# Attention and a routed expert layer on one core: the expert slots written out in place of a loop, and the router's logits computed transposed in four column strips

## The reference

```python
# attention: 16 heads of 16 channels, causal, on layernorm(x) and ctx
qp, kp = elu(q) + 1, elu(k) + 1
out[t] = qp[t] @ sum_{s <= t} outer(kp[s], v[s])      # per head
x = x + (out / cumsum(qp)) @ Wo + bo
# router and experts on layernorm(x), called hidden
h      = relu(hidden @ W1 + b1)          # 256 -> 128
logits = h @ W2 + b2                     # 128 -> 8
sel    = argmax(softmax(logits))         # one expert per token
x      = x + hidden @ expert_W[sel] + expert_b[sel]
```

## Time and profile before

| | before |
|---|---|
| median of 3 runs | 1158.4 us |
| the profiled execution: span | 1158.5 us |
| first part, to the last `place` | 0 to 943 us |
| tables for the slots | 943 to 960 us |
| slots | 960 to 1158.5 us |
| busy over the span | PE 90%, DVE 73%, POOL 51%, ACT 49% |

### The profile page before, as it was taken

How to read it: one execution, slowest core, us unless ns; L and a number is a source line. 1 busy time by engine, 2 the same in 40 slices (tenths; PEclk the granted TensorE clock), 3 DMA queues, 4 the chain that set the end, 5 groups by cost and what they waited for, 6 DMA issues and landing times.

```text
span 1158.5 us, 39374 instructions
## 1 busy us (share of the span) xinstructions
PE 1044.3 (90%) x15828; PEld 727.5 (63%) x15829; DVE 843.8 (73%) x1739; ACT 562.7 (49%) x945; POOL 587.0 (51%) x682
## 2 busy tenths in 40 slices
PE   2989999999999999999999999999999626999996
PEld 1666666666666666666667666666667414666664
DVE  2688887887888887878878788888877643555554
ACT  2544544454555544554455545445444114666664
POOL 4144444544444455554555444544444444777766
PEclk9989999999999999999999999999999857999999
DMA  3823333333333333333334333333322014666664
GB/s 104 241 75 93 94 93 94 93 93 93 94 93 95 97 97 97 101 101 100 107 104 120 97 93 93 93 93 93 93 76 76 30 51 138 193 190 184 195 185 135
DMA packets 88601, 127.11 MB, mean 110 GB/s; under 512 B 13693, under 2 KB 67584, under 8 KB 88320
## 3 DMA queue, kind: packets, MB, share of 16 engines
q1 hardware_dynamic: 75392, 89.98, 30.1%
q0 software_dynamic: 13056, 34.90, 7.9%
HBM read 73.03 MB, written 36.06 MB: 94 GB/s over the span
## 4 chain that ended last, share of the span: by engine, by line
PE 23%; issue 23%; POOL 18%; DMA 13%; SPq 7%; ACT 5%; DVE 4%; DVEq 0%; POOLq 0%; ACTq 0%
DMA x_res<-in_x 8%; PE b_a L808 8%; POOL buckets L409 7%; PE b_b L1014 6%; SPq L338 5%; POOL x_res L433 3%; DMA stage<-buckets 2%; DMA out<-stage 2%; PE b_b L855 2%; PE b_a L1005 2%; ACT x2n L494 2%; POOL row L419 2%; PE b_a L803 2%; PE b_b L813 2%; ACT x2T L506 1%
## 5 line engine op out<-in xcount | busy, mean ns | idle before, releaser
L581 DVE TENSOR_TENSOR stage<-b_s,causal 128x1024 f32<-128x1024 f32 x192 | 226.1, 1219 | 47.6 <-PE b_s L835 37.1
L461 POOL DMA_INDIRECT out<-stage x136 | 136.6, 1005 | 59.2 <-issue 30.2
L409 POOL DMA_INDIRECT buckets<-row,place x128 | 140.8, 1100 | 34.6 <-issue 34.6
L1014 PE MATMUL b_b<-we_sb,x3T 128*128 x544 | 150.5, 400 | 0.0
L808 PE MATMUL b_a<-xnT,wq_sb 128*128 128x512 f32 x256 | 128.0, 624 | 7.4 <-ACT x2T L506 5.1
L539 ACT ACTIVATE x3n<-stage 128x256 f32<-128x256 f32 x136 | 81.5, 599 | 88.4 <-DMA stage<-buckets 83.8
L813 PE MATMUL b_b<-wo_sb,attT 128*128 128x256 f32 x512 | 121.4, 391 | 2.4 <-DVE attT L681 2.4
L494 ACT ACTIVATE x2n<-row 128x256 f32<-128x256 f32 x128 | 66.5, 590 | 115.5 <-POOL row L425 115.5
L407 POOL TENSOR_TENSOR onehots<-onehots,onehot 128x32 bf16<-128x32 bf16 x32 | 7.8, 244 | 223.6 <-DVE place L614 223.6
L808 PE MATMUL b_a<-ctxT,wk_sb 128*128 128x512 f32 x256 | 118.4, 605 | 1.8 <-ACT pos L480 1.8
L813 PE MATMUL b_b<-wv_sb,ctxT 128*128 128x256 f32 x512 | 119.0, 385 | 0.0
(11 more groups left out here) (119 smaller groups left out, 1954.4 us busy)
## 6 DMA issues: line engine op xcount, KB each, us to landing
stage<-buckets SPq DMA_DIRECT2D x136, 130.0 KB, 2.2
x_in<-in_x SPq DMA_DIRECT2D x32, 512.0 KB, 5.1
ctxT<-in_ctx SPq DMA_DIRECT2D x32, 512.0 KB, 6.3
qsel<-qp SPq DMA_DIRECT2D x256, 64.0 KB
x_res<-in_x SPq DMA_DIRECT2D x32, 512.0 KB, 7.3
out<-stage POOLq DMA_INDIRECT x136
we_sb<-in_L_ffn_expert_W SPq DMA_DIRECT2D x8, 256.0 KB, 6.0
buckets<-row,place POOLq DMA_INDIRECT x128
```

Source lines behind the costliest of these rows:

```text
L409: pool.indirect_dma_start(buckets, bass.IndirectOffsetOnAxis(place[:, slot(route), t:t + 1], 0), row[:, slot(route), t, :], None).then_inc ...
L461: pool.indirect_dma_start(out.rearrange("t p n -> (t p) n"), bass.IndirectOffsetOnAxis(rows2[:, r, TOKEN:TOKEN + 1].bitcast(U32), 0), sums ...
L581: dve.tensor_tensor(dst.rearrange("p g h s q -> p g (h s) q"), b_s[:, :, 256 * t:256 * t + 256].rearrange("p g (a q) -> p g a q", q=C), ca ...
L1014: last = pe.matmul(b_b[:, h, 0:D], x3T[:, h, P * k:P * k + P], we_sb[:, k, bass.ds(e, 1), :], start=(k == 0), stop=(k == KC - 1))
```

## The change

1. The loop over slots becomes a straight program: the same `step` calls, with plain numbers where the loop variable was. Registers with the slots' rows and experts are still read eight at a time.
2. The router's second product is turned round. `w2_wide` (8 columns of W2 and 24 columns of zeros) is the stationary operand, `hT` of a tile the moving one, and the four tiles go to the four strips of 32 PSUM partitions. ACT adds the bias on the way to `logitsT`, PE transposes that once (128x128) between the two halves of `wo`, and DVE takes maximum and marks straight from PSUM, without its bias add.
3. Around it: `b2` is loaded as four columns of 8 rows, behind the experts' weights; two memsets and one copy on DVE build `bias_2` and `w2_wide`.

```diff
         def slot_schedule(eng, step, begin=lambda first, how_many: None):
-            begin((0, -2), RING)
-            for j in range(RING):
-                step(*((0, j - k) if j - k >= 0 else None for k in range(3)))
-            with eng.Fori(1, SLOTS // RING, 1) as i:
-                begin((i, -2), RING)
-                for v in range(RING):
-                    step(*((i, v - k) for k in range(3)))
-            begin((SLOTS // RING, -2), 2)
-            for j in range(SLOTS, SLOTS + 2):
-                step(*((j // RING, j % RING - k) if j - k < SLOTS else None for k in range(3)))
+            for j in range(SLOTS + 2):
+                if j % RING == 0:
+                    begin((j // RING, -2), RING if j < SLOTS else 2)
+                step(*(((j - k) // RING, (j - k) % RING) if 0 <= j - k < SLOTS else None for k in range(3)))
...
+                sp.wait_ge(s_cst, MADE)
+                for t in range(GT):
+                    sp.dma_start(bias_2[R * t:R * t + E, :], b2.rearrange("(n o) -> n o", o=1)).then_inc(s_eld, 16)
...
+                if merge:
+                    act.wait_ge(s_lg, n(merge, k=1))
+                    if group_no(merge) == 0:
+                        act.wait_ge(s_eld, EXPERTS)
+                    else:
+                        act.wait_ge(s_lgTp, n(merge))
+                    act.activation(logitsT[:, :], b_s[:, 0, 0:P], ACT.Identity, bias=bias_2[:, :]).then_inc(s_lgT, 1)
...
+            dve.tensor_copy(w2_wide[:, 0:E], w2_sb[:, :]).then_inc(s_w2, 1)
...
-                        dve.wait_ge(s_pick, n(merge, 5))
-                    dve.wait_ge(s_lg, n(merge, k=1))
-                    dve.tensor_tensor(logits[:, :, :], b_s[:, 0, 0:GT * E].rearrange("p (t e) -> p t e", e=E),
-                                      per_expert(bias_2[:, :]), ALU.add).then_inc(s_pick, 1)
-                    dve.wait_ge(s_pick, n(merge, 5, 1))
-                    dve.tensor_reduce(top[:, :], logits[:, :, :], axis=AX.X, op=ALU.max).then_inc(s_pick, 1)
+                        dve.wait_ge(s_pick, n(merge, 4))
+                    dve.wait_ge(s_lgTp, n(merge, k=1))
+                    scored = b_s[:, 0, P:2 * P].rearrange("p (t e) -> p t e", e=R)[:, :, 0:E]
+                    dve.tensor_reduce(top[:, :], scored, axis=AX.X, op=ALU.max).then_inc(s_pick, 1)
...
             def logit_products():
                 for t in range(GT):
-                    last = pe.matmul(b_s[:, 0, E * t:E * t + E], hT[:, P * t:P * t + P], w2_sb[:, :],
+                    last = pe.matmul(b_s[strip(t), 0, 0:P], w2_wide[:, :], hT[:, P * t:P * t + P],
                                      start=True, stop=True)
                 return last
...
-                if attend:
-                    for b in range(2):
+                for b in range(2):
+                    if attend:
                         pe.wait_ge(s_att, n(attend, 2, 1 + b))
                         for t in range(b, GT, 2):
                             last = tokens_first(b_b[:, b, D * (t // 2):D * (t // 2) + D], attT, wo_sb, t)
                         last.then_inc(s_y, 1)
+                    if merge and b == 0:
+                        pe.wait_ge(s_lgT, n(merge, k=1))
+                        pe.transpose(b_s[:, 0, P:2 * P], logitsT[:, :], ident[:, :]).then_inc(s_lgTp, 1)
```

More of the change, by code:

```diff
@@ L37, in build @@
     RING = 8
-    WEIGHTS = 16 * 14
-    EXPERTS = 16 * (E + 1)
+    WEIGHTS = 16 * 13
+    EXPERTS = 16 * (E + 1 + GT)
     POOL_MADE = 22
-    MADE = 12
+    MADE = 14
     FILL_STEPS = E + 3 + 3 * (E - 1) + 4
@@ L79, in build @@
         bias_1 = sb("bias_1", [FF, 1])
-        bias_2 = sb("bias_2", [P, E])
+        bias_2 = sb("bias_2", [P, 1])
         bias_e = sb("bias_e", [P, E, D])
@@ L87, in build @@
         w2_sb = sb("w2_sb", [FF, E])
+        w2_wide = sb("w2_wide", [FF, R])
         we_sb = sb("we_sb", [P, KC, E, D])
@@ L117, in build @@
         hT = sb("hT", [FF, N])
+        logitsT = sb("logitsT", [P, P])
         logits = sb("logits", [P, GT, E])
@@ L203, in build @@
         s_hT = sem("s_hT")
+        s_w2 = sem("s_w2")
         s_lg = sem("s_lg")
+        s_lgT = sem("s_lgT")
+        s_lgTp = sem("s_lgTp")
         s_pick = sem("s_pick")
@@ L298, in load_weights @@
                                      b[P * k:P * k + P].rearrange("(p o) -> p o", o=1)).then_inc(s_wld, 16)
-                for dst, b, wide in ((bias_v, bv, D), (bias_o, bo, D), (bias_2, b2, E)):
+                for dst, b, wide in ((bias_v, bv, D), (bias_o, bo, D)):
                     sp.dma_start(dst[:, :],
@@ L567, in _ @@
             dve.memset(slot_e[:, :], 0.0).then_inc(s_cst, 1)
+            dve.memset(bias_2[:, :], 0.0).then_inc(s_cst, 1)
+            dve.memset(w2_wide[:, :], 0.0).then_inc(s_cst, 1)
             dve.wait_ge(s_cst, MADE)
             dve.wait_ge(s_wld, WEIGHTS)
+            dve.tensor_copy(w2_wide[:, 0:E], w2_sb[:, :]).then_inc(s_w2, 1)
             def of_mask(which):
@@ L686, in step @@
                     if group_no(merge) >= 1:
-                        dve.wait_ge(s_pick, n(merge, 5))
-                    dve.wait_ge(s_lg, n(merge, k=1))
-                    dve.tensor_tensor(logits[:, :, :], b_s[:, 0, 0:GT * E].rearrange("p (t e) -> p t e", e=E),
-                                      per_expert(bias_2[:, :]), ALU.add).then_inc(s_pick, 1)
-                    dve.wait_ge(s_pick, n(merge, 5, 1))
-                    dve.tensor_reduce(top[:, :], logits[:, :, :], axis=AX.X, op=ALU.max).then_inc(s_pick, 1)
-                    dve.wait_ge(s_pick, n(merge, 5, 2))
-                    dve.tensor_tensor(tied[:, :, :], logits[:, :, :], per_tile(top[:, :]), ALU.is_equal)\
-                        .then_inc(s_pick, 1)
-                    dve.wait_ge(s_pick, n(merge, 5, 3))
+                        dve.wait_ge(s_pick, n(merge, 4))
+                    dve.wait_ge(s_lgTp, n(merge, k=1))
+                    scored = b_s[:, 0, P:2 * P].rearrange("p (t e) -> p t e", e=R)[:, :, 0:E]
+                    dve.tensor_reduce(top[:, :], scored, axis=AX.X, op=ALU.max).then_inc(s_pick, 1)
+                    dve.wait_ge(s_pick, n(merge, 4, 1))
+                    dve.tensor_tensor(tied[:, :, :], scored, per_tile(top[:, :]), ALU.is_equal).then_inc(s_pick, 1)
+                    dve.wait_ge(s_pick, n(merge, 4, 2))
                     dve.tensor_tensor(logits[:, :, :], tied[:, :, :], per_expert(iota_m8[:, :]), ALU.mult)\
                         .then_inc(s_pick, 1)
-                    dve.wait_ge(s_pick, n(merge, 5, 4))
+                    dve.wait_ge(s_pick, n(merge, 4, 3))
                     dve.tensor_reduce(first[:, :], logits[:, :, :], axis=AX.X, op=ALU.min).then_inc(s_pick, 1)
-                    dve.wait_ge(s_pick, n(merge, 5, 5))
+                    dve.wait_ge(s_pick, n(merge, 4, 4))
                     if group_no(merge) >= 1:
@@ L795, in _ @@
             pe.wait_ge(s_wld, WEIGHTS)
+            pe.wait_ge(s_w2, 1)
             def strip(g):
```

## The result

| | time (us) | before on the same chip | ratio, 95% interval |
|---|---|---|---|
| changed kernel | 1171.5 | 1158.5 | 1.0107, 1.0087 to 1.0128 |

The changed kernel is slower by 13 us; its profiled execution took 1171.0 us, with a span of 1169.2. The forecast was 1162.5, 9 us too low, with the time inside the range of 1154 to 1174: + 4 was said and + 13 came.

What follows compares the result with a forecast made beforehand. The prediction took a closed chain through PE, DVE and POOL to bound each step. From 1158.5 us, + 0.5 (first merge) + 5.6 (28 steps) - 2 (slots) gave 1162.6, stated as 1162.5, range 1154 to 1174.

Steps and rivals of the forecast that it cites:

- rival B: Steps: no pull on POOL, L425 stays 8.29 us behind `place`, 0.51 us lost per step; 1171 us, chance 0.18.
- A's steps: Steps in the forecast's own case: masks and `kp` pull POOL forward, 0.20 us lost each; 1159 to 1166, chance 0.50.
- F: Slots: streamed instructions stall the engines beside full DMA queues, 1.4 us per 8 slots; 1185, or 1174 at half; chance 0.09.
- The closed chain: Steps: each waits in a ring from `attT` through `wo`, `row`, `place`, POOL, `x2n` and attention sums to `attT`; 27.8 us.
- The late `qp`: Steps: `qp` 1.4 us later also delays SP's DMAs and moves `x_res` for POOL's L433; costed at nothing.
- The saving on PE swallowed by `attT`: Logits on PE: PE free 0.6 us earlier, but `wo` then waits for `attT`; gain 0 to 0.1 us, taken as 0.
- The rule of the Trainium skill: Logits on PE: swap operands and tile by columns when the moving side has 32 columns or fewer; 18 us in all.
- `place` 0.51 us late: DVE in a step: transpose behind half of `wo` delays `top`, `qp` and both `row` adds; `place` at 433.44 instead of 432.93.
- `kp` pulls POOL forward: DVE and POOL: masks and `kp` start only 0.20 us later, so L425 and `x2n` come 0.20 us later, not 0.51.
- 28 x 0.20 = 5.6 us: First part: each of 28 steps gets 0.20 us longer, 5.6 us in all; bounds per step 0.11 and 0.51.
- The slots, - 2 us: Slots: dropping the loop's jumps saves 0.3 us at 15 borders, half reaching POOL; about 2 us, bounds 0 and 7.8.

Runs made afterwards that it cites:

- eight more operations: Kernel before plus eight small chained DVE operations, output unused, behind `onehot` and ahead of `qp` in each step: 1205.1 us against 1189.8.
- two turns: Kernel before with its slot loop over 16 slots instead of 8, leaving out every second jump back: 1158.7 us against 1159.6.
- the router's half: Changed kernel with the old loop over slots put back: 1198.6 us against 1189.8 before, and 1198.9 against 1189.4 on a second chip.
- the straight half: Kernel before with only its slots written out straight: 1182.8 us against 1189.8, 1183.3 against 1189.4, and 1163.8 against 1159.6 on three chips.
- the one with `kp` later: Kernel before with the first `kp` of a step moved behind the second masks on DVE: 1203.2 us against 1189.8.

## Why the prediction was right or wrong

- **The number.** + 13 came where + 4 was forecast. The first part lost 7.9 us for a forecast of 5.6, and the slots lost 4.7 where they were to win 2. The 1171.5 measured is what rival B gives (1171), but that is luck: B says that the scale stays 8.29 us behind `place`, and it came to 7.82. What happened is A's steps and, for the slots, something of F.
- **The closed chain** of `attT`, `wo`, `row`, `place`, POOL, `x2n` was right: a usual step is longer by what its parts changed, + 0.62 and - 0.47, and the remaining 14.13 us did not move. The late `qp` cost nothing, as taken, though it did move POOL's L435 by 1.9 us (446.23): there it runs beside the whole of `u`, which takes 3.13 us instead of 1.73, and DVE still has 1.60 us to wait for PE ahead of `attT`.
- **The saving on PE swallowed by `attT`** was right: 0.62 us less for the logits, and PE's idle time before `wo` 15.1 us over 32 steps, where before had 2.4. The rule of the Trainium skill (TensorEngine Tiling (Array Packing), "Performance Considerations") was worth 18 us in the prediction, 0.6 us a step; PE's own time for the logits did fall, from 1.05 to 0.43 us, but PE wasn't what the step waited for.
- **`place` 0.51 us late**: 0.62, all of the difference ahead of `top`. It started 2.96 us behind `attT`, where I had 2.84: `wo` 0.75 behind `attT` (0.80), the transpose 1.83 behind that (1.71), `top` 0.38 behind its start (0.33).
- **`kp` pulls POOL forward**: right, and stronger, 0.47 instead of 0.31. The run with eight more operations shows the same 1.07 us DMA with the old router, so this is shown and not only argued. POOL's DMA ended 1.49 us behind the start of `kp`, as the prediction had read from two steps.
- **28 x 0.20 = 5.6 us**: 7.9, and 9.3 to 10.8 on the other kind of chip. The usual step lost 0.15 or 0.16 (there 0.19), less than taken, so 4.4 us; what I left out is that a step which falls out of the pattern is moved as well. The two short steps of before, in which `kp` starts just behind the fourth DMA (0.06 and 0.38 us) and leaves it at 0.96 us, vanished (1.5 us), and longer ones appeared (1.9 us). The forecast took one step for 28, and came near the 7.9 partly because one error made up for the other.
- **The slots, - 2 us**: this is the step that failed, by its sign. The term was 15 borders x 0.3 us x 0.5. The borders gave more than it said: DVE's stalls fell by 0.63 us each (1.05 to 0.42), and yet the slots got 4.7 us longer. So the half that was to reach POOL did not, or was lost under a cost that the sum put at nothing. What the jumps alone are worth stays open: 8 of them fewer should have given 1.2 us, and two turns gave 1158.7 against 1159.6, which can't be told from 1.2 nor from 0. The cost is something like rival F, at a fifth of its price (17 x 1.4 = 24 us), but the engines didn't stand for their instructions: rows of the slots came late behind packets of code, of which one of 16 KB arrives for every 16 slots or so.
- The Trainium skill (Runtime: NRT & Kernel Launch, "Instruction fetch mechanics") says that crossing into the next block of straight code is mostly hidden, and warns of the taken branch. For the engines the trace agrees: DVE's border stalls fell by 10 us. For the kernel it was the other way round on this kind of chip, most likely because the fetch shares the DMA engines with a stage whose rows come by them (their busy share is 0.56 to 0.59 there).

The link from packet to late slot rests on their coming together in the traces of three straight kernels and on the absence of all but one or two in the two loops; no run changed the number of packets in a straight program, so it is argued and not shown. That the straight program wins 5 to 7 us on chips 1 and 2 is measured twice and not explained. There the slots take 217 to 231 us, with or without the loop: the usual distance of two output DMAs is 1.43 us instead of 1.29, and every sixth or so is over 2 us, where the faster kind has one to eight such in all. The straight programs fetch their packets there as well (7 or 8 of 16 KB), but the rows are seldom what ACT stands for; in the waits view of the router's half, 965 to 1165 us:

```profile
PEld b_b L1033 <- issue: 51.8, 43, 3.2
ACT x3n L554 <- DMA stage<-buckets: 11.0, 15, 2.4
```

and of the straight half:

```profile
PEld b_b L1008 <- issue: 40.9, 45, 2.9
ACT x3n L533 <- DMA stage<-buckets: 24.0, 28, 1.9
```

PE stands 41 to 52 us for nothing that these traces show (4 on chip 3), and some of its records are missing. Three kernels with the loop have more of it (50 to 52) than the four straight ones (41 to 46), which would fit the gain, but the one with `kp` later has the loop and 41.6.

No version that ran beats before on both kinds of chip; the router with its transpose behind a quarter of `wo` and the slots in the loop was not tried (its 28 steps were 1.8 us longer than those of before on the faster kind, so no gain is to be expected there). On chips like those of the first two sets it is the straight slots with the old router (1183); on the others the kernel before.

## What to carry to other kernels

Before an engine is given less work, find in one step what it would wait for next: here `attT` was ready at the same moment, and 0.6 us of PE's time bought a longer step. A transpose on the way to a serial chain belongs where its input becomes ready, not at the next tidy border between two blocks: moving it ahead by a quarter or by half of `wo` gave back most of what the 28 steps had lost. And straight code may not be free where the DMA engines carry the stage: count the instruction packets in that window, and look at what lands late behind them.

## What I had not expected

- Two kinds of chip: before takes 1158 to 1160 us on two, 1189 to 1190 on the other two, although the first part is faster on the latter. POOL's L425 comes 8.28 us behind `place` on the first kind and 7.80 on the second, and the step is 27.84 and 27.37 us. The difference is one small operation, `nr` on POOL: 0.68 us where it runs beside DVE's second `kp`, 0.20 where DVE's masks, and with them that `kp`, come 1.4 us later. The masks wait for PE's products of that half; these start 3.95 us behind `place` on both kinds and have ended when `kp` has, but on the slower kind DVE starts the masks 1.3 us after that. Why stays open.
- DVE's two `kp` operations (two operands in SBUF each) thus cost POOL twice in a step, 0.5 us at the fourth DMA and 0.48 us at `nr`, on the chain that sets the step. How narrow this is shows in the short step of before at 127 us: `kp` starts 0.06 us behind the fourth DMA instead of 0.01, and the DMA takes 0.96 us instead of 1.49.
- The start of the first `place` varies between 94.3 and 101.1 us from one profiled execution to the next (94.7 and 99.5 for the kernel before), so a single pair of spans can't be read to better than some 3 us; differences within the steps can.
